# A gated windowed-attention and stream-mixing kernel: TensorE's chunk laid out anew, scores and values in the middle of a unit, the division one unit later, output parts in halves, gelu's low part on GpSimd and the normalisation on ScalarE

## The chip, the cores and the metric

One core of one Trainium2 chip runs the whole program. The metric is the device time in microseconds of one execution; a few executions of the same kernel are timed, and one more is recorded by the hardware profiler.

## What is computed

The input x is 8 x 512 x 2048 (batch, channels, positions). In short:

```
x = x + tanh(g_xattn) * attention(layernorm(x), ctx, mask)
x = x + tanh(g_ffn)  * mix(layernorm(x))
```

Attention works in windows of 128 positions: q and k from the normalised x, v from ctx (512 channels to 256), 8 heads of 32, softmax over 128 keys, exact gelu on the result, then a projection back to 512 channels. The mixing part takes each row's 2048 positions as four streams of 512. From 24 logits per row it makes a softmax for reading (pre), a softmax for writing (post) and, by 50 Sinkhorn iterations on a 4 x 4 matrix in logarithms, a mixing matrix. The output is the mixed streams plus post times the product of the read stream with a 512 x 512 matrix.

```
def step(carry, _):
    u, v = carry
    u = -jax.nn.logsumexp(Z + v[..., None, :], axis=-1)
    v = -jax.nn.logsumexp(Z + u[..., :, None], axis=-2)
```

## The kernel before

**Tiles and steps.** A chunk G is 512 positions of one batch element (32 chunks). It has four windows of two head groups each, which makes eight units. One batch element is a stage of 32 units, and there are 256 units in all. Every engine runs its own hand-written program, a loop over steps g with one unit per step; what stands in a step is set by tables of offsets within the chunk (`NORM_AT`, `HI_X_AT`, `LOW_X_AT`, `HI_CTX_AT`, `LOW_CTX_AT`, `T_AT`, ...). r is the step's number in its chunk, 0 to 7. Engines meet only through semaphores, and each engine works strictly in the order written.

**One unit.** TensorE makes the scores of unit g (`scores`, into the one bank `s_ps`), then the transposed scores less the maximum of unit g-1 (`scores_t`, bank `st_ps`), then the values of unit g-2 (`values`, bank `av_ps`), then the step's large products through a ring of four PSUM banks (`banked_at`). VectorE takes the maximum (`maximum`, L1003); ScalarE the exponential (`exp_scores`, L806) and the reciprocal of the denominator as exp(-ln) (`inverse_den`, L813 and L815); VectorE divides (`divide`, L1011). `values` of a unit waits for the division of the unit before it.

**Precision by halves.** The bf16 operands are pairs of a high and a low part. ScalarE makes the high part of x and ctx (`hi_x`, `hi_ctx`), GpSimd the low part by a subtraction (`split_x` L473, `split_ctx` L478); GpSimd also normalises x in place (`norm_x` L467). The high part of gelu's result is ScalarE's (`hi_gelu`), the low part VectorE's (`low_gelu` L1027). q and k are copied by 24 DMAs of the SP queue per chunk into stacked tiles `q_st` and `k_st`, before the chunk's first scores.

**The balance (Sinkhorn).** For a finished batch element, 98 half iterations run beside the units of the next one, up to four per step: VectorE sums `kp` and takes the reciprocal (`half_iteration`, L1135 and L1136), GpSimd multiplies `ke` by it into `kp` (`scale`, L533), VectorE sums again. In a step the four halves are spread between VectorE's other work: the maximum stands ahead of half 0; the reads of banks, the division and gelu's low part between halves 0 and 1; the output parts between 1 and 2; mask and statistics between 2 and 3. In GpSimd's program `split_x` stands between its scales 0 and 1, `norm_x` between 1 and 2, `split_ctx` between 2 and 3.

**The output.** 32 tiles of 128 rows. A tile's rows are reloaded (`load_x1t`), the read stream is made by ScalarE and three VectorE operations (`make_xpre`, L1168), transposed and multiplied on TensorE (`transpose_pre`, `branch`, L729), and the output tile `otile` is built: ScalarE's first products (`first_out`), three streams added for each of four columns (`add_stream`, L1180, two operations together), and the branch (`add_y`, L1193, four together). There is one `otile`; `first_out` waits until the tile before is stored. A tile starts every eight steps, from `TILE_AT`, also in the tail behind the last unit.

```
if 0 <= g < NU:
    scores(g)
if 0 <= g - 1 < NU:
    scores_t(g - 1)
if 0 <= g - 2 < NU:
    values(g - 2)
for what in banked_at(g):
    bank_free(what)
```

## Time and profile before

| what | value |
|---|---|
| median of 3 runs | 1891.67 us (1890.44 to 1893.29) |
| the profiled execution's own time | 1890.67 us |
| its span | 1888.8 us |
| TensorE busy | 1383.0 us, 73% |
| VectorE busy | 1437.9 us, 76% |
| ScalarE busy | 945.7 us, 50% |
| GpSimd busy | 824.0 us, 44% |
| first and last maximum (first and last unit on VectorE) | 68.5 us, 1595.7 us |

Busy time is the union of an engine's instructions, so an instruction that stands still while it waits for a port counts as busy. The profile's names: PE is TensorE, PEld its weight loads, DVE VectorE, ACT ScalarE, POOL GpSimd, SP the engine whose queue issues most DMAs. An arrow in brackets behind a row names what ended the engine's idle time before it.

### The profile page before, as it was taken

The numbers are of one execution on the slowest core, as the hardware profiler recorded it, in microseconds if no ns is written. First come the engines' busy times: TensorE is split into PE (matmuls) and PEld (weight loads), VectorE is DVE, ScalarE is ACT, GpSimd is POOL, SyncE is SP. The second block draws the span as 40 slices with busy tenths as digits, with TensorE's granted clock in tenths as the row PEclk, the third lists the DMA queues.
The fourth block names the chain that finished last, engine by engine and source line by source line (L and its number), as shares of the span: only waits on it lengthen the run. The fifth ranks groups of instructions, "written<-read, shape, count | busy, mean of one in ns | idle before, by whom it ended". The sixth has DMA issues, their size and how long they took to land. (4 is left out here: it accounts for less than half of the span.)

```text
span 1888.8 us, 35318 instructions
## 1 busy us (share of the span) xinstructions
PE 1383.0 (73%) x12301; PEld 848.2 (45%) x12448; DVE 1437.9 (76%) x3684; ACT 945.7 (50%) x1889; POOL 824.0 (44%) x1397
## 2 busy tenths in 40 slices
PE   2788999889978787888888887878888876431133
PEld 0555656556544454545544454445454544210011
DVE  3344555777788888888888888888788888777789
ACT  2445675555655555554655565554655554321112
POOL 4433334555454544555455545555464523323210
PEclk9889999989999999999999899999999997665567
DMA  7456765566666666666666666666655443421123
GB/s 248 145 146 184 207 192 159 161 175 180 174 180 183 185 165 170 187 189 169 176 173 182 169 190 176 177 171 178 171 169 150 134 120 93 121 73 60 56 89 123
DMA packets 173985, 299.80 MB, mean 159 GB/s; under 512 B 23664, under 2 KB 74736, under 8 KB 169712
## 3 DMA queue, kind: packets, MB, share of 16 engines
q1 hardware_dynamic: 156400, 263.97, 44.8%
q0 software_dynamic: 17408, 33.56, 11.1%
q8 instruction: 100, 1.64, 0.3%
q14 instruction: 77, 0.63, 0.1%
HBM read 179.75 MB, written 67.11 MB: 131 GB/s over the span
## 5 line engine op out<-in xcount | busy, mean ns | idle before, releaser
L533 POOL TENSOR_TENSOR kp<-ke,sv 128x64 f32<-128x64 f32 x376 | 183.4, 488 | 299.9 <-DVE sv L1136 299.8
L1135 DVE TENSOR_REDUCE ssum<-kp 128x16 f32<-128x64 f32 x768 | 181.8, 237 | 172.0 <-POOL kp L533 166.6
L533 POOL TENSOR_TENSOR kp<-ke,sa 128x64 f32<-128x64 f32 x392 | 125.8, 321 | 358.9 <-DVE sa L1136 358.9
L806 ACT ACTIVATE probs<-st_ps,key_bias 128x512 f32<-128x512 f32 x256 | 174.3, 681 | 199.6 <-PE st_ps L703 193.8
L605 PE MATMUL pr<-x_hl,wk 128*128 128x512 bf16 x736 | 194.2, 419 | 64.6 <-DVE k_hl L983 63.8
L1003 DVE TENSOR_REDUCE negm<-s_ps 128x4 bf16<-128x512 f32 x256 | 167.7, 655 | 75.6 <-PE s_ps L689 73.0
L605 PE MATMUL pr<-x_hl,wq 128*128 128x512 bf16 x707 | 187.0, 411 | 44.8 <-POOL x_hl L473 38.1
L473 POOL TENSOR_TENSOR x_hl<-xc,x_hl 128x512 bf16<-128x512 f32 x128 | 156.3, 1222 | 134.2 <-ACT x_hl L774 133.7
L619 PE MATMUL pr<-wv,ctx_hl 128*128 128x256 bf16 x1536 | 190.8, 284 | 24.0 <-POOL ctx_hl L478 24.0
L478 POOL TENSOR_TENSOR ctx_hl<-ctx_raw,ctx_hl 128x512 bf16<-128x512 f32 x128 | 176.4, 1378 | 57.4 <-ACT ctx_hl L768 57.4
L689 PE MATMUL s_ps<-k_st,q_st 97*128 97x128 bf16 x1024 | 102.8, 224 | 112.6 <-DVE negm L1003 101.0
L632 PE MATMUL pr<-o_sb,wo 128*128 128x512 bf16 x714 | 177.2, 386 | 4.1 <-issue 1.3
L619 PEld LDWEIGHTS pr<-wv,ctx_hl 128*128 128x128 bf16 x1536 | 152.3, 102 | 58.1 <-issue 36.1
L689 PEld LDWEIGHTS s_ps<-k_st,q_st 97*128 97x128 bf16 x1024 | 74.1, 100 | 189.8 <-DVE negm L1003 124.4
L701 PE MATMUL st_ps<-q_st,k_st 96*128 96x128 bf16 x1024 | 150.0, 223 | 7.3 <-ACT probs L806 4.4
L605 PEld LDWEIGHTS pr<-x_hl,wk 128*128 128x128 bf16 x768 | 79.3, 106 | 158.2 <-DVE k_hl L983 63.0
L703 PE MATMUL st_ps<-id_bf,negm 128*128 128x128 bf16 x1024 | 149.4, 223 | 0.0
L1011 DVE TENSOR_TENSOR o_sb<-av_ps,rden 128x128 f32<-128x128 f32 x256 | 70.4, 275 | 103.3 <-ACT rden L815 102.8
L716 PE MATMUL av_ps<-probs,v_t 128*32 128x128 f32 x2048 | 111.9, 290 | 41.0 <-DVE o_sb L1011 39.7
L605 PEld LDWEIGHTS pr<-x_hl,wq 128*128 128x128 bf16 x768 | 75.0, 104 | 141.3 <-issue 39.9
L729 PE MATMUL f<-wb,xpt 128*128 128x512 f32 x256 | 132.0, 664 | 8.5 <-ACT xpt L885 8.5
L676 PE MATMUL pr<-id_sb,xpre 128*128 128x128 f32 x128 | 24.1, 321 | 154.3 <-DVE xpre L1168 154.3
(139 smaller groups left out, 3031.7 us busy)
## 6 DMA issues: line engine op xcount, KB each, us to landing
xs<-in_dram SPq DMA_DIRECT2D x128, 256.0 KB, 4.0
xc<-in_dram SPq DMA_DIRECT2D x32, 1024.0 KB, 5.9
ctx_raw<-in_dram SPq DMA_DIRECT2D x32, 1024.0 KB, 5.1
x1c<-in_dram POOLq DMA_DIRECT2D x64, 512.0 KB, 5.9
x_dram<-x1c SPq DMA_DIRECT2D x32, 1024.0 KB, 4.3
out_dram<-otile SPq DMA_DIRECT2D x64, 512.0 KB, 5.0
q_st<-q_hl SPq DMA_DIRECT2D x384, 64.0 KB
k_st<-k_hl SPq DMA_DIRECT2D x384, 64.0 KB
```

What stands on the lines that cost most here:

```text
L473: nc.gpsimd.tensor_tensor(x_hl[:, G % 2, 1, t, :], xc[:, t, :], x_hl[:, G % 2, 0, t, :], ALU.subtract).then_inc(x_split, 1)
L478: ins = nc.gpsimd.tensor_tensor(ctx_hl[:, 1, t, :], ctx_raw[:, t, :], ctx_hl[:, 0, t, :], ALU.subtract)
L533: nc.gpsimd.tensor_tensor(kp[:], ke[:], v, ALU.mult).then_inc(kp_made, 1)
L605: ins = nc.tensor.matmul(bank(what)[:], w[:, a, t, i * P:(i + 1) * P], x_hl[:, G % 2, m, t, :], start=(t == 0 and a + m == 0), stop=(t == ...
L619: ins = nc.tensor.matmul(bank(what)[:, j * E:(j + 1) * E], ctx_hl[:, a, t, win], wv[:, m, t, :], start=(t == 0 and a + m == 0), stop=(t == ...
L632: ins = nc.tensor.matmul(bank(what)[:], wo[:, a, et, t * P:(t + 1) * P], o_part(G, et, m), start=(et == 0 and a + m == 0), stop=(et == ET ...
L689: ins = nc.tensor.matmul(s_ps[:, h * W:(h + 1) * W], q_st[0:ROWS + 1, G % 2, et, h, win], k_st[0:ROWS + 1, G % 2, et, h, win], start=True, ...
L701: nc.tensor.matmul(part, k_st[0:ROWS, G % 2, et, h, win], q_st[0:ROWS, G % 2, et, h, win], start=True, stop=False)
L703: ins = nc.tensor.matmul(part, negm[:, k % 2, h:h + 1].broadcast_to([P, P]), id_bf[:], start=False, stop=True)
L806: nc.scalar.activation(probs[:, k % 2, :], st_ps[:], ACT.Exp, bias=key_bias[:, b % 2, w:w + 1], scale=SCALE).then_inc(exp_done, 1)
L1003: nc.vector.tensor_reduce(negm[:, k % 2, :], s_ps[:].rearrange("p (h j) -> p h j", h=HPT), AX.X, ALU.max, negate=True).then_inc(max_done, 1)
L1135: cf.link(nc.vector.tensor_reduce(s_t, k, AX.X, ALU.add))
```

## The change

- **TensorE.** In a step `scores_t(g - 1)` comes first, then the first large product, then `scores(g + 1)` (a unit earlier than before) and `values(g - 2)`, then the other products. `branch` is two halves in two steps, `select` two halves in two steps. The transposes of x1 move from r = 2, 3 to 3, 4, the logits from 4 to 7, the transposes of the read stream from 3 to 1, the branch from 4 to 5 and 6.
- **VectorE.** `divide` is for unit g-3 and stands ahead of the bank reads. `add_stream` is one column at a time: one operation between halves 1 and 2, one between 2 and 3; `add_y` two and two; `make_xpre` two and one. `low_gelu` goes. The mask rows are made once for all chunks.
- **GpSimd.** `split_x` moves from between scales 0 and 1 to between 1 and 2; `norm_x` goes to ScalarE, ahead of each `hi_x`; `low_gelu` comes in at r = 3, one part ahead of scale 2 and one ahead of scale 3. The tables put `split_ctx` at r = 0, 1, 1, 4 (before 1, 2, 3, 5), and its first three parts now in steps in which ScalarE makes high parts of ctx too (0, 0, 1, 1).
- **ScalarE.** `norm_x` as above; `inverse_den` behind the first bank read.
- **Output and tail.** Two `otile` buffers. The tiles of the first six batch elements start one step later than before in the chunk; those of the last two start every six steps, with a denser table (`BEHIND`). The Sinkhorn steps begin one step later.
- **SP queue.** `store_x1` moves from r = 0 to 1; the separate mask loads of each stage go.

```diff
-NORM_AT, HI_X_AT, LOW_X_AT = [2, 3, 4, 5], [3, 4, 5, 6], [4, 5, 6, 7]
-HI_CTX_AT, LOW_CTX_AT = [0, 0, 1, 4], [1, 2, 3, 5]
-
-T_AT, LOGITS_AT, SELECT_AT = [2, 2, 3, 3], 4, 6
-STAT_B_AT = [2, 4]
+HI_X_AT, LOW_X_AT = [1, 4, 5, 6], [2, 5, 6, 7]
+HI_CTX_AT, LOW_CTX_AT = [0, 0, 1, 1], [0, 1, 1, 4]
+
+T_AT, LOGITS_AT, SELECT_AT = [3, 3, 4, 4], 7, 8
+STAT_B_AT = [1, 3]
...
+BESIDE = dict(load=-8, first=-6, xpre=-5, pre=-4, branch_0=0, branch_1=1, out_0=-1, out_1=0,
+              stream_1=0, stream_2=1, y=2, stream_3=4, pair_1=5, pair_2=6, pair_3=7, store_0=5, store_1=8)
+BEHIND = dict(load=-5, first=-3, xpre=-3, pre=-2, branch_0=-1, branch_1=-1, out_0=-1, out_1=0,
+              stream_1=0, stream_2=1, y=2, stream_3=3, pair_1=3, pair_2=4, pair_3=5, store_0=4, store_1=6)
+LAST_BESIDE = B - 3
+TILE_AT = {(f, t): UNITS * (f + 1) + 53 + UPC * t for f in range(LAST_BESIDE + 1) for t in range(DT)}
+TILE_AT.update({(B - 2, t): NU + SINK_AT - 1 + 6 * t for t in range(DT)})
+TILE_AT.update({(B - 1, t): NU + SINK_AT + len(SINK) + 1 + 6 * t for t in range(DT)})
...
             for g in range(FIRST, LAST):
-                if 0 <= g < NU:
-                    scores(g)
                 if 0 <= g - 1 < NU:
                     scores_t(g - 1)
-                if 0 <= g - 2 < NU:
-                    values(g - 2)
-                for what in banked_at(g):
-                    bank_free(what)
+                made = banked_at(g)
+                for n, what in enumerate(made):
...
+                    if n == 0:
+                        if 0 <= g + 1 < NU:
+                            scores(g + 1)
+                        if 0 <= g - 2 < NU:
+                            values(g - 2)
...
+                scale_at(f, its, 1)
                 for H, t in at_step(g, -2, LOW_X_AT):
                     split_x(H, t)
-                scale_at(f, its, 1)
-                for H, t in at_step(g, -2, NORM_AT):
-                    norm_x(H, t)
+                if 0 <= G - 1 < NG and r == 3:
+                    low_gelu(G - 1, 0)
                 scale_at(f, its, 2)
+                if 0 <= G - 1 < NG and r == 3:
+                    low_gelu(G - 1, 1)
...
+            def output_parts(g, half):
+                for j in range(1, N):
+                    for done, t in tiles_at(g, f"stream_{j}"):
+                        add_stream(done, t, j, half)
+                for done, t in tiles_at(g, "y"):
+                    add_y(done, t, half)
+                for j in range(1, N):
+                    for done, t in tiles_at(g, f"pair_{j}"):
+                        add_stream(done, t, j, 2 + half)
+                for done, t in tiles_at(g, "xpre"):
+                    make_xpre(done, t, half)
```

**Where the order moves.** TensorE, step r = 4 of a chunk in a steady stage, before (line numbers of the kernel before; L716 and L720 are the values, L659 the logits, L632 the output projection, L729 the whole branch, L689 the next unit's scores):

```order
L703 MATMUL st_ps<-id_bf,negm 128x128
L716 MATMUL av_ps<-probs,v_t 32x128 x4
L720 MATMUL av_ps<-probs,ones 32x128 x4
L659 MATMUL pr<-xt,wf 32x512 x4
L632 MATMUL pr<-o_sb,wo 128x512 x12
L729 MATMUL f<-wb,xpt 128x512 x4
L689 MATMUL s_ps<-k_st,q_st 128x128 x4
```

and changed, the end of step 4's transposed scores left out, steps 5 and 6 (L637 the output projection, L697 scores, L724 and L728 values, L739 the branch, L624 v):

```order
L637 MATMUL pr<-o_sb,wo 128x512 x6
L697 MATMUL s_ps<-k_st,q_st 128x128 x4
L724 MATMUL av_ps<-probs,v_t 32x128 x4
L728 MATMUL av_ps<-probs,ones 32x128 x4
L637 MATMUL pr<-o_sb,wo 128x512 x6
L739 MATMUL f<-wb,xpt 128x512 x2
```

The branch is cut in two and has left the step that also held the logits; scores and values now stand behind the step's first product.

VectorE, step r = 4, before: the halves of the balance are L1135 and L1136, both columns of a stream (L1180) stand in one gap, and mask row (L996) and statistics (L1044) in the next:

```order
L1003 TENSOR_REDUCE negm<-s_ps 128x4
L1135 TENSOR_REDUCE ssum<-kp 128x16
L1136 RECIPROCAL sa<-ssum 128x16
L983 SCALAR_TENSOR_TENSOR k_hl<-pr,bk_sb,k_hl 128x512
L1011 TENSOR_TENSOR o_sb<-av_ps,rden 128x128
L1135 TENSOR_REDUCE ssum<-kp 128x16
L1136 RECIPROCAL sv<-ssum 128x16
L1180 SCALAR_TENSOR_TENSOR otile<-x1t_even,cmat,otile 128x512 x2
L1135 TENSOR_REDUCE ssum<-kp 128x16
L1136 RECIPROCAL sa<-ssum 128x16
L996 TENSOR_SCALAR neg_row<-maskbc 1x512
L1044 BN_STATS bn_b<-x1c 128x6 x2
```

and changed (L1160 and L1161 the halves, L1207 the stream, L1005 a piece of the next element's statistics):

```order
L1034 TENSOR_REDUCE negm<-s_ps 128x4
L1160 TENSOR_REDUCE ssum<-kp 128x16
L1161 RECIPROCAL sa<-ssum 128x16
L1042 TENSOR_TENSOR o_sb<-av_ps,rden 128x128
L1019 SCALAR_TENSOR_TENSOR k_hl<-pr,bk_sb,k_hl 128x512
L1160 TENSOR_REDUCE ssum<-kp 128x16
L1161 RECIPROCAL sv<-ssum 128x16
L1207 SCALAR_TENSOR_TENSOR otile_even<-x1t_even,cmat,otile_even 128x512
L1160 TENSOR_REDUCE ssum<-kp 128x16
L1161 RECIPROCAL sa<-ssum 128x16
L1207 SCALAR_TENSOR_TENSOR otile_even<-x1t_even,cmat,otile_even 128x512
L1005 BN_STATS bn_a<-xs 128x6
```

The pair of stream operations is now one in each of two gaps, and the division comes ahead of the bank read.

GpSimd, the end of step r = 1 and steps 2 and 3, changed (L536 is the scale of the balance, L476 the low part of ctx, L471 that of x, L482 that of gelu):

```order
L476 TENSOR_TENSOR ctx_hl<-ctx_raw,ctx_hl 128x512 x2
L536 TENSOR_TENSOR kp<-ke,sa 128x64
L536 TENSOR_TENSOR kp<-ke,sv 128x64
L536 TENSOR_TENSOR kp<-ke,sa 128x64
L471 TENSOR_TENSOR x_hl<-xc,x_hl 128x512
L536 TENSOR_TENSOR kp<-ke,sv 128x64
L536 TENSOR_TENSOR kp<-ke,sa 128x64
L536 TENSOR_TENSOR kp<-ke,sv 128x64
L536 TENSOR_TENSOR kp<-ke,sa 128x64
L482 TENSOR_TENSOR o_sb<-g_sb,o_sb 128x512
L536 TENSOR_TENSOR kp<-ke,sv 128x64
L482 TENSOR_TENSOR o_sb<-g_sb,o_sb 128x512
```

Two parts of ctx now stand together in the last gap of step 1; the part of x has moved one scale later, behind scale 1; gelu's two parts each stand ahead of a scale in step 3.

## Rows read from the trace of the kernel before

**Rows 1.** The page: span, and busy time of each engine.

```profile
span 1888.8 us, 35318 instructions
PE 1383.0 (73%) x12301; PEld 848.2 (45%) x12448; DVE 1437.9 (76%) x3684; ACT 945.7 (50%) x1889; POOL 824.0 (44%) x1397
```

**Rows 2.** Windows: steady stages (20 chunks), tail; columns PE, PEld, DVE, ACT, POOL busy.

```profile
576.00:1596.00 1020.00, 828.68 (x7528) 507.58 (x7624) 867.16 (x2253) 573.48 (x1151) 501.54 (x840) 0.94 0.60 168
1596.00:1889.00 293.00, 87.50 (x263) 43.31 (x264) 230.32 (x583) 58.10 (x97) 65.05 (x172) 0.61 0.26 86
```

**Rows 3.** Waits of VectorE, 576 to 1596 us: total us, times, longest.

```profile
DVE ssum L1135 <- POOL kp L533: 84.2, 138, 1.7
DVE o_sb L1011 <- ACT rden L815: 33.1, 28, 2.4
DVE negm L1003 <- PE s_ps L689: 4.4, 10, 1.1
```

**Rows 4.** Groups by line, whole run: busy us, mean ns, idle before.

```profile
L478 POOL TENSOR_TENSOR ctx_hl<-ctx_raw,ctx_hl 128x512 bf16<-128x512 f32 x128 | 176.4, 1378 | 57.4 <-ACT ctx_hl L768 57.4
L473 POOL TENSOR_TENSOR x_hl<-xc,x_hl 128x512 bf16<-128x512 f32 x128 | 156.3, 1222 | 134.2 <-ACT x_hl L774 133.7
L1027 DVE TENSOR_TENSOR o_sb<-g_sb,o_sb 128x512 bf16<-128x512 f32 x64 | 44.4, 735 | 4.6 <-ACT o_sb L831 4.6
L996 DVE TENSOR_SCALAR neg_row<-maskbc 1x512 bf16<-1x512 f32 x32 | 17.9, 560 | 0.4 <-issue 0.2
L774 ACT ACTIVATE x_hl<-xc 128x512 bf16<-128x512 f32 x128 | 79.4, 621 | 6.5 <-POOL xc L467 6.4
```

**Rows 5.** Timeline of VectorE, 1802 to 1804 us: two halves with nothing between.

```profile
1802.12 0.26 DVE L1135 TENSOR_REDUCE ssum<-kp 128x16 f32<-128x64 f32 x1 [0.41 <-POOL kp L533]
1802.42 0.25 DVE L1136 RECIPROCAL sv<-ssum 128x16 f32<-128x16 f32 x1
1804.00 0.27 DVE L1135 TENSOR_REDUCE ssum<-kp 128x16 f32<-128x64 f32 x1 [0.41 <-POOL kp L533]
```

**Rows 6.** Timeline, 851 to 854 us: VectorE's stream pair first, GpSimd behind.

```profile
851.16 1.37 DVE L1180 SCALAR_TENSOR_TENSOR otile<-x1t_even,cmat,otile 128x512 f32<-128x512 f32 x2
851.33 0.65 POOL L533 TENSOR_TENSOR kp<-ke,sv 128x64 f32<-128x64 f32 x1 [0.19 <-DVE sv L1136]
851.94 1.60 POOL L478 TENSOR_TENSOR ctx_hl<-ctx_raw,ctx_hl 128x512 bf16<-128x512 f32 x1
```

**Rows 7.** Timeline, 903 to 906 us: GpSimd's large operation first.

```profile
903.29 1.16 POOL L478 TENSOR_TENSOR ctx_hl<-ctx_raw,ctx_hl 128x512 bf16<-128x512 f32 x1
903.73 1.94 DVE L1180 SCALAR_TENSOR_TENSOR otile<-x1t_odd,cmat,otile 128x512 f32<-128x512 f32 x2
```

**Rows 8.** Timeline of ScalarE and VectorE around gelu, 317 to 323 us.

```profile
317.32 1.28 ACT L819 ACT_TABLE_LOAD   x1
321.43 0.67 ACT L806 ACTIVATE probs<-st_ps,key_bias 128x512 f32<-128x512 f32 x1
322.51 1.13 ACT L831 ACTIVATE o_sb<-g_sb 128x512 bf16<-128x512 f32 x2
322.64 0.29 DVE L1011 TENSOR_TENSOR o_sb<-av_ps,rden 128x128 f32<-128x128 f32 x1 [4.17 <-ACT rden L815]
```

**Rows 9.** Timeline of TensorE, 289 to 299 us: select and v in one step.

```profile
289.58 4.40 PE L668 MATMUL pr<-sti,lgs 128*128 128x32 f32 x32
293.79 5.31 PE L619 MATMUL pr<-wv,ctx_hl 128*128 128x256 bf16 x24
```

**Rows 10.** Timeline of VectorE, tail: `add_y` beside the balance (two), behind it (two).

```profile
1709.44 2.63 DVE L1193 SCALAR_TENSOR_TENSOR otile<-f,post,otile 128x512 f32<-128x512 f32 x4
...
1748.66 2.63 DVE L1193 SCALAR_TENSOR_TENSOR otile<-f,post,otile 128x512 f32<-128x512 f32 x4
...
1837.46 2.73 DVE L1193 SCALAR_TENSOR_TENSOR otile<-f,post,otile 128x512 f32<-128x512 f32 x4 [0.34 <-PE f L729]
...
1851.23 2.73 DVE L1193 SCALAR_TENSOR_TENSOR otile<-f,post,otile 128x512 f32<-128x512 f32 x4 [0.22 <-PE f L729]
```

More of the change, by code:

```diff
@@ L661, in logits, with select @@
                 ins.then_inc(bank_full, 1)
-            def select(what):
+            def select(what, part):
                 kind, f, i = what
-                pe.wait_ge(lg_copied, NC * (f + 1))
-                for t in range(DT):
+                if part == 0:
+                    pe.wait_ge(lg_copied, NC * (f + 1))
+                for t in (2 * part, 2 * part + 1):
                     for w in range(NC):
@@ L1188, in add_y @@
[L1188 to L1199 removed]
+                if half:
+                    ins.then_inc(xpre_ready, 1)
```

284 lines of the change are left out of this document (143 added, 141 removed).

## The prediction

> **What bounds the kernel now.** I read the page first [rows 1]: no engine is full, VectorE is the busiest with 76% and TensorE next with 73%, so the limit differs by stage and has to be read there. The windows [rows 2] show two regimes. From 576 to 1596 us (chunks 11 to 30, every engine at work) VectorE is busy 867.2 of 1020 us. That is 43.4 us per chunk of 51.0, with 7.6 us idle. GpSimd is busy 501.5, so neither it nor ScalarE (573.5) is near full. The tail, from 1596 us, has only VectorE busy, 230.3 of 293 us. The waits of VectorE in the steady part [rows 3] say what the 7.6 us are: 84.2 us (4.2 per chunk) for GpSimd's scale of the balance, 33.1 us (1.7) for ScalarE's reciprocal before the division, and only 4.4 us for TensorE's scores. So the bound is VectorE together with its ping-pong with GpSimd. TensorE waits for them, and a smoother TensorE gives time only where it paces: in the first chunks.
>
> **The ping-pong.** With nothing between, two halves take 1804.00 - 1802.12 = 1.88 us [rows 5], of which 0.41 each is idle. Work of VectorE in the gap behind a half is free up to about 0.4 us. A large GpSimd operation ahead of the scale costs where VectorE has too little to cover it.
>
> **Two engines, one port.** Where VectorE's stream pair comes first, GpSimd's part of ctx takes 1.60 us and ends 1.01 us after the pair [rows 6]. Where GpSimd comes first it takes 1.16, and the pair 1.94 instead of 1.37 [rows 7], though VectorE had nothing else in hand. So a stream operation, which reads two tiles from SBUF, and a large GpSimd operation do not run together. The Trainium skill (SBUF — State Buffer, Who interferes with whom) says that a VectorE instruction with two SBUF inputs contends with a GpSimd one that reads SBUF, and that the loser fully blocks. By that rule the trace agrees: 1.60 against 1.16 us.
>
> **The change, part by part, per steady chunk.**
>
> *Work that VectorE loses.* Two low parts of gelu of 0.735 us and one mask row of 0.56 [rows 4]: 2.0 us by duration. Successive instructions overlap by about 0.1 each, so I take 1.65. Left: 43.4 - 1.65 = 41.75. The streams, the read stream and the branch are the same operations, only parted.
>
> *Waits that go.* The division is for unit g-3, so ScalarE has a whole unit more: the 1.7 us go. The part of x (1.16 to 1.22) leaves the gap that holds only the division or a bank read, and the normalisation leaves GpSimd. That is most of today's 4.2 us, and I count all of it anew.
>
> *Waits that come*, in a chunk with the balance in all eight steps. Gaps that now hold the division alone, r = 7 and 0: 0.3 each. The scale that starts behind a single stream operation must let it finish: about 0.15 in five gaps, 0.75. Part of x behind a short bank read, r = 2: it ends about 0.5 after the stream operation wants the port, 0.5. At r = 5 and 6 two bank reads cover it, at r = 7 the branch reads PSUM. Part of ctx at r = 4, now ahead of a stream operation: 0.65. DMA issue at r = 6: 0.1. Then three places where GpSimd takes what ScalarE makes in the same step, which it did not before. At r = 0 the high part of ctx stands on ScalarE behind exponential, bank read and reciprocal, each of which waits for TensorE; I put its end 5.5 us into the step, where GpSimd wants it at 4.0, and with the port 1.65 in all. At r = 1 two parts stand together, the second made about 6.0 us into the step, 2.05. At r = 3 the low part of gelu: table loads, gelu and exponential take 322.10 - 317.32 = 4.8 us, the first high part 0.6 more [rows 8]; begun 2.7 us into step 2 (5.7 us long), that is about 8.1, where GpSimd wants it at 7.1; with the port and the second part 1.95. Sum 0.6 + 0.75 + 0.5 + 0.65 + 0.1 + 1.65 + 2.05 + 1.95 = 8.25. The balance runs in 26 of 32 steps, which makes 6.7; 0.7 for the softmax steps and what else waits now. Together 7.4, against 7.6 today.
>
> Step lengths and ScalarE's times in it are my placement; no row shows them. Bounds: ScalarE is in time everywhere (3.4 less at full, 2.8 on the mean), or each of the three is later by another 0.8 us (a reciprocal and a bank read), 2.0 more on the mean. I take the middle because step r = 3 shows today that ScalarE falls behind by 4.17 us at the gelu [rows 8].
>
> *Steady sum:* 41.75 + 7.4 = 49.15 against 51.0, -1.85 per chunk. Chunks 8 to 31, 24 of them: **-44 us**.
>
> *ScalarE* gets four normalisations per chunk; the nearest row is its copy of the same shape, 0.62 us [rows 4]: 2.5 us of 51, from 56% busy [rows 2] to about 62%. Nothing for them, since none stands at r = 2 or 3; if that cover went, they would delay the exponential by 1.2 us at their steps. *SP queue:* the q and k stacks must be there half a unit earlier, behind the load of a tile and `store_x1` a step later. TensorE waits for scores inputs nowhere in [rows 3] beyond 4.4 us; zero. *PSUM ring and branch halves:* zero in the steady part, TensorE has 828.7 of 1020 us [rows 2].
>
> *First eight chunks* (TensorE paces from the second to the sixth). Select 4.40 and v 5.31 us stand in one step there [rows 9]; halves of select in two other steps give back about 4 once. The wait of 4.17 us at gelu [rows 8] shrinks by perhaps 1 per chunk, since values now stand later in the step. **-10 us**, between 0 and -25.
>
> *Tail.* Beside the balance a tile takes 1748.66 - 1709.44 = 39.2 us in eight steps [rows 10], now six steps, each with more in it; the balance runs its own steps at the pace of [rows 5] whatever else stands there, and single stream operations hide a little more of the 0.41 us. A tile of the second last element that stood behind the balance is now beside it: nothing to -5 us. Against it, at the end: today ten stream operations lie between read stream and branch and TensorE is awaited for 0.22 to 0.34 us [rows 10]; now eight do, 1.43 us less cover, three times: +4.5. And the balance begins a step later: +4. **+6 us**, between -10 and +15.
>
> Sum: 1890.67 - 44 - 10 + 6 = 1842.7 for the profiled execution; the median stands 1.0 above it: **1844 us**.
>
> **Rivals.**
>
> *The port and ScalarE decide, slower.* A chunk has ten large GpSimd operations: four of x, four of ctx, two of gelu. I charge 3.1 us of blocking for them. If each blocks the operation that VectorE has next by 0.7 us (its 1.16 less the 0.45 of a half), that is 7.0: +3.9 per chunk, x 24 = +94, **1938 us**. It decides from +2.0 per chunk, 0.5 us for each of the ten. For it: the pair of 1.94 us [rows 7], and that one of the two streams now stands in every gap behind which GpSimd works. Against: at r = 5, 6 and 7 there is cover. The Trainium skill (Perfetto Trace Analysis, Optimizing Scalar/DVE Operations) warns that moving operations between VectorE and GpSimd might not help, since they share a read port; it speaks against gelu's low part on GpSimd.
>
> *The waits nearly vanish.* ScalarE is in time and the ports overlap well: 3.4 us per chunk of waits instead of 7.4. -4.0 x 24 = -96: **1748 us**. For it: today 7.6 us of idle time come from a few gaps. Against: at least 2.1 us of what I list hang on no placement.
>
> *A wash.* The steady chunk keeps its 51.0 because what goes returns elsewhere: -10 + 6, **1888 us**. For it: 7.4 against 7.6 is nearly that already, and VectorE's lost 1.65 us may only bare a wait for GpSimd, for gelu's low part covers one today.
>
> **How the numbers follow.** Forecast (1810 to 1878) 0.52, slower by the port 0.18, waits vanish 0.16, wash 0.14. The range takes the unknowns: 24 x 2.8 = 67 below and 24 x 2.0 = 48 above, with the tail: 1785 to 1900. It leaves out most of the slower rival and the far part of the fast one, together under 0.2. Differences under 0.2% (3.8 us) can't be told from none. Of the wash 0.06 is faster, 0.06 the same, 0.02 slower: faster 0.74, same 0.06, slower 0.20.
>
> **What would show it.** VectorE's wait for ScalarE's reciprocal gone from its list; its wait for the scale about 6 us per chunk and longest at r = 0, 1 and 3; GpSimd waiting for ScalarE's high part of ctx and of gelu; VectorE busy about 42 us per chunk; a steady chunk of 49 us; 1.5 us waits for the branch in the last three tiles. Wrong if TensorE is what VectorE waits for in the steady part, if the chunk stays at 51, or if it falls below 47.

## The result, and the profile after

The changed kernel takes **1884.14 us** (median of 5 runs, 1878.06 to 1888.89), the kernel before 1891.1 in the same comparison: ratio 0.9947, interval 0.9925 to 0.9969. That is 10 us less by the ratio, where 47 were forecast. The profiled execution took 1878.06 us, the fastest of the five and 6 us under their median, so terms of a few us below are not sure. Of run 7 below, one of six executions took 4650.91 us; its ratio leaves that one out. Where the time lies, by the first maximum of a unit: the first maximum comes 2.5 us later (71.0 for 68.5), chunks 0 to 7 take 307.8 us against 318.8 (-11.0, forecast -10), chunks 8 to 31 take 1201.4 against 1208.4 (**-7.0, forecast -44**), and from the last maximum to the end it is 296.0 against 293.1 (+2.9, forecast +6). So one term failed, the steady one.

The page of the changed kernel (its first lines), answering to [rows 1]:

```profile
span 1876.2 us, 35394 instructions
PE 1423.7 (76%) x12448; PEld 859.5 (46%) x12448; DVE 1390.8 (74%) x3582; ACT 1055.6 (56%) x2017; POOL 799.5 (43%) x1333
```

VectorE lost 47 us of work, ScalarE gained 110, and TensorE's busy time rose by 41 us though it computes the same (147 matmul records of large products are missing from the trace of before, but an output product with one missing is busy 2.77 us there and a whole one 2.76, so they explain little of that). For the steady part I take chunks 8 to 27, the same 20 chunks in every kernel from here on. The windows view, before (first line) and after (second); columns: time, PE, PEld, DVE, ACT, POOL busy, TensorE's granted clock, DMA share, GB/s:

```profile
387.30:1406.60 1019.30, 837.15 (x7648) 513.83 (x7744) 853.59 (x2248) 578.68 (x1168) 517.19 (x871) 0.95 0.63 176
```

```profile
378.80:1388.10 1009.30, 866.38 (x7750) 521.97 (x7749) 823.93 (x2178) 647.29 (x1244) 495.50 (x831) 0.93 0.62 177
```

VectorE's work fell by 29.7 us, 1.48 per chunk (forecast 1.65). Its idle time rose from 165.7 to 185.4 us, that is from 8.3 to 9.3 per chunk. What it waits for there (total, times, longest), answering to [rows 3]:

```profile
DVE ssum L1160 <- POOL kp L536: 120.1, 187, 4.3
DVE ssum L1160 <- ACT ke L892: 21.0, 10, 3.2
DVE q_hl L1019 <- ACT q_hl L819: 8.2, 5, 2.4
...
DVE o_sb L1042 <- ACT rden L846: 1.4, 2, 1.2
```

The wait for the reciprocal is gone, as forecast (36.7 us before in the same chunks). The wait for the scale has grown from 89.4 us, and it is one place: ahead of the fourth half of step r = 1 VectorE stands idle 3.09 us in the mean of the 15 such steps that hold the balance; it is 1.16 at r = 0 (15 steps) and 1.46 ahead of the third half at r = 3 (10 steps). Of GpSimd, ScalarE and TensorE (same view, same chunks) these have grown or are new:

```profile
ACT lnden L844 <- PE av_ps L728: 122.5, 108, 3.2
...
POOL ctx_hl L476 <- ACT ctx_hl L792: 113.4, 38, 6.1
PE s_ps L697 <- DVE negm L1034: 107.8, 68, 3.2
POOL o_sb L482 <- ACT o_sb L862: 77.0, 20, 7.8
```

Before, TensorE's wait for the maximum was 77.3 us and ScalarE's for the values 18.8. In exchange ScalarE's wait for the transposed scores fell from 118.6 to 12.5, and TensorE's for VectorE's read of q and k, 55.1 before, is gone. Both engines wait less in sum (TensorE is idle 142.9 us instead of 182.1), but elsewhere. Read from the bottom of the chain: VectorE waits for GpSimd, GpSimd for ScalarE, ScalarE for TensorE, and TensorE for VectorE. One step r = 1 shows the whole ring (the timeline; start, length, engine; in brackets idle time before and its releaser):

```profile
929.40 0.63 PE L684 MATMUL pr<-id_sb,xpre 128*128 128x128 f32 x4 [0.69 <-DVE xpre L1195]
...
931.35 0.63 DVE L1034 TENSOR_REDUCE negm<-s_ps 128x4 bf16<-128x512 f32 x1
...
932.03 0.61 PE L697 MATMUL s_ps<-k_st,q_st 97*128 97x128 bf16 x4 [2.00 <-DVE negm L1034]
...
932.67 0.65 PE L724 MATMUL av_ps<-probs,v_t 128*32 128x128 f32 x8
...
933.55 0.66 DVE L1207 SCALAR_TENSOR_TENSOR otile_even<-x1t_even,cmat,otile_even 128x512 f32<-128x512 f32 x1
...
933.69 5.09 PE L610 MATMUL pr<-x_hl,wq 128*128 128x512 bf16 x12
...
934.33 1.15 POOL L476 TENSOR_TENSOR ctx_hl<-ctx_raw,ctx_hl 128x512 bf16<-128x512 f32 x1
...
934.83 1.20 DVE L1207 SCALAR_TENSOR_TENSOR otile_even<-x1t_even,cmat,otile_even 128x512 f32<-128x512 f32 x1
...
938.82 0.69 ACT L819 ACTIVATE q_hl<-pr,bq_sb 128x512 bf16<-128x512 f32 x1 [4.39 <-PE pr L610]
...
939.08 2.75 PE L610 MATMUL pr<-x_hl,wk 128*128 128x512 bf16 x12
939.40 1.14 ACT L792 ACTIVATE ctx_hl<-ctx_raw 128x512 bf16<-128x512 f32 x2
940.10 1.17 POOL L476 TENSOR_TENSOR ctx_hl<-ctx_raw,ctx_hl 128x512 bf16<-128x512 f32 x1 [4.62 <-ACT ctx_hl L792]
...
941.55 0.27 DVE L1160 TENSOR_REDUCE ssum<-kp 128x16 f32<-128x64 f32 x1 [4.33 <-POOL kp L536]
```

At r = 1 the first bank product is only the read stream's transposes. Behind them stand the scores of the next unit, which need the maximum of this one, since both use the one tile `s_ps`. TensorE stands idle 2.00 us until VectorE starts the step. Only then come values and the q product, ScalarE's read of it 7.5 us into the step (938.82 - 931.35), the high part of ctx behind that, GpSimd's low part, the scale, and VectorE's half. The step takes 10.7 us. The q product takes 5.09 us where the k product behind it, of the same shape, takes 2.75. The granted clock says why (windows view):

```profile
929.50:930.60 1.10, 0.53 (x4) 0.28 (x4) 0.36 (x1) 1.10 (x3) 1.10 (x2) 1.00 1.09 207
930.60:931.35 0.75, 0.00 (x0) 0.00 (x0) 0.44 (x3) 0.33 (x1) 0.24 (x1) 1.00 0.39 77
931.35:932.00 0.65, 0.00 (x0) 0.00 (x0) 0.65 (x3) 0.00 (x0) 0.30 (x1) 0.71 0.02 3
932.00:933.69 1.69, 1.63 (x21) 1.01 (x21) 1.62 (x7) 0.00 (x0) 0.30 (x1) 0.50 0.43 164
933.69:938.60 4.91, 4.91 (x16) 1.78 (x13) 3.31 (x6) 0.59 (x2) 1.76 (x2) 0.52 0.92 317
939.08:941.80 2.72, 2.72 (x15) 1.08 (x12) 0.24 (x1) 2.69 (x5) 1.42 (x2) 1.00 0.01 3
```

Full level (2.4 GHz) before the idle time, a fall within it, half (1.2 GHz) behind it and through nearly all of the q product. In the mean of the 20 chunks the clock is 0.86 at r = 1 and 0.73 at r = 3 (before: 0.95 and 0.84).

### The profile page after: what moved, and what is told of

Its sections match the earlier page's. It is cut to its first block, busy times and chain, and to the rows that moved or that the text cites. A ratio compares the mean times of both kernels' runs of the same rounds, so it can differ in the third digit from the quotient of the medians.

```text
span 1876.2 us, 35394 instructions
## 1 busy us (share of the span) xinstructions
PE 1423.7 (76%) x12448; PEld 859.5 (46%) x12448; DVE 1390.8 (74%) x3582; ACT 1055.6 (56%) x2017; POOL 799.5 (43%) x1333
## 4 chain that ended last, share of the span: by engine, by line
PE 43%; DVE 22%; POOL 11%; ACT 10%; issue 9%; DMA 2%; SPq 2%; DVEq 0%; POOLq 0%; ACTq 0%
PE pr L610 11%; PE pr L624 7%; PE pr L637 6%; POOL kp L536 5%; PE f L739 4%; DVE ssum L1160 4%; PE av_ps L724 4%; POOL ctx_hl L476 3%; DVE otile_odd L1207 3%; DVE negm L1034 2%; PE av_ps L728 2%; SPq L404 2%; DVE sa L1161 2%; PE s_ps L697 2%; DVE sv L1161 1%
## 5 line engine op out<-in xcount | busy, mean ns | idle before, releaser
L1160 DVE TENSOR_REDUCE ssum<-kp 128x16 f32<-128x64 f32 x768 | 181.8, 237 | 208.3 <-POOL kp L536 206.1
L536 POOL TENSOR_TENSOR kp<-ke,sa 128x64 f32<-128x64 f32 x392 | 158.0, 403 | 283.8 <-DVE sa L1161 283.8
L536 POOL TENSOR_TENSOR kp<-ke,sv 128x64 f32<-128x64 f32 x376 | 166.2, 442 | 226.7 <-DVE sv L1161 225.7
L476 POOL TENSOR_TENSOR ctx_hl<-ctx_raw,ctx_hl 128x512 bf16<-128x512 f32 x128 | 149.6, 1174 | 217.3 <-ACT ctx_hl L792 217.3
L610 PE MATMUL pr<-x_hl,wq 128*128 128x512 bf16 x768 | 205.8, 426 | 35.1 <-POOL x_hl L471 35.1
L1034 DVE TENSOR_REDUCE negm<-s_ps 128x4 bf16<-128x512 f32 x256 | 167.0, 652 | 74.7 <-PE s_ps L697 73.2
L697 PE MATMUL s_ps<-k_st,q_st 97*128 97x128 bf16 x1024 | 104.4, 226 | 151.3 <-DVE negm L1034 138.4
L637 PE MATMUL pr<-o_sb,wo 128*128 128x512 bf16 x768 | 188.0, 389 | 8.8 <-POOL o_sb L482 6.6
L471 POOL TENSOR_TENSOR x_hl<-xc,x_hl 128x512 bf16<-128x512 f32 x128 | 148.5, 1160 | 92.8 <-ACT x_hl L805 92.8
L624 PE MATMUL pr<-wv,ctx_hl 128*128 128x256 bf16 x1536 | 183.0, 277 | 3.1 <-DVE wv L1244 3.1
L844 ACT ACTIVATE lnden<-av_ps 128x128 f32<-128x128 f32 x256 | 71.0, 277 | 196.5 <-PE av_ps L728 191.4
L697 PEld LDWEIGHTS s_ps<-k_st,q_st 97*128 97x128 bf16 x1024 | 71.7, 100 | 221.7 <-DVE negm L1034 153.4
L624 PEld LDWEIGHTS pr<-wv,ctx_hl 128*128 128x128 bf16 x1536 | 148.7, 99 | 28.3 <-issue 9.8
L1207 DVE SCALAR_TENSOR_TENSOR otile_even<-x1t_even,cmat,otile_even 128x512 f32<-128x512 f32 x192 | 147.8, 780 | 1.6 <-ACT otile_even L925 1.2
L1207 DVE SCALAR_TENSOR_TENSOR otile_odd<-x1t_odd,cmat,otile_odd 128x512 f32<-128x512 f32 x192 | 148.4, 795 | 0.7
L724 PE MATMUL av_ps<-probs,v_t 128*32 128x128 f32 x2048 | 117.1, 302 | 36.1 <-DVE o_sb L1042 35.2
L739 PE MATMUL f<-wb,xpt 128*128 128x512 f32 x256 | 138.8, 677 | 5.5 <-ACT xpt L916 5.5
## 6 DMA issues: line engine op xcount, KB each, us to landing
xc<-in_dram SPq DMA_DIRECT2D x32, 1024.0 KB, 10.7
```

The lines of the kernel that those rows point to most:

```text
L476: ins = nc.gpsimd.tensor_tensor(ctx_hl[:, 1, t, :], ctx_raw[:, t, :], ctx_hl[:, 0, t, :], ALU.subtract)
L536: nc.gpsimd.tensor_tensor(kp[:], ke[:], v, ALU.mult).then_inc(kp_made, 1)
L610: ins = nc.tensor.matmul(bank(what)[:], w[:, a, t, i * P:(i + 1) * P], x_hl[:, G % 2, m, t, :], start=(t == 0 and a + m == 0), stop=(t == ...
L624: ins = nc.tensor.matmul(bank(what)[:, j * E:(j + 1) * E], ctx_hl[:, a, t, win], wv[:, m, t, :], start=(t == 0 and a + m == 0), stop=(t == ...
L637: ins = nc.tensor.matmul(bank(what)[:], wo[:, a, et, t * P:(t + 1) * P], o_part(G, et, m), start=(et == 0 and a + m == 0), stop=(et == ET ...
L697: ins = nc.tensor.matmul(s_ps[:, h * W:(h + 1) * W], q_st[0:ROWS + 1, G % 2, et, h, win], k_st[0:ROWS + 1, G % 2, et, h, win], start=True, ...
```

## The experiments

Each run is told as median, ratio to the kernel before in the same comparison, and interval. Theory A took the handover within a step for the cause, as the forecast had it; TensorE's order came in with run 7. A gap is the part of VectorE's step between two halves of the balance, and its wait is the idle time ahead of the half that ends it. Differences between runs are of medians; by the ratios they are the same within 4 us. A number for a gap or a clock by step is the mean over the steps of that r in the 20 chunks (for gaps, over those that hold the balance).

### 1. The parts of ctx a step later

```diff
-HI_CTX_AT, LOW_CTX_AT = [0, 0, 1, 1], [0, 1, 1, 4]
+HI_CTX_AT, LOW_CTX_AT = [0, 0, 1, 1], [1, 2, 4, 5]
```

> Changed kernel with GpSimd's low parts of ctx at r = 1, 2, 4, 5 instead of 0, 1, 1, 4, so that none waits for a high part that ScalarE makes in the same step. Theory A (handover in the same step): in the changed kernel VectorE waits about 3.1 us in one gap of r = 1 and 1.2 in one of r = 0, and GpSimd waits 113 us for the high part of ctx in 20 chunks. This takes about 2.5 us per chunk away and gives 0.7 back at the new places: -1.8 x 24 = -43, about 1841 us. Theory B (the time lost there is slack that the next wait takes, TensorE's order or ScalarE's answers): 1875 to 1888 us, VectorE's wait for the scale falls but another wait grows.

**1827.98 us**, 0.9649 (0.9637 to 0.9662): 56 us faster than the changed kernel. Its waits in the 20 chunks:

```profile
DVE ssum L1160 <- POOL kp L536: 60.2, 159, 2.6
...
POOL ctx_hl L476 <- ACT ctx_hl L792: 30.4, 5, 6.1
...
DVE ssum L1160 <- ACT ke L892: 19.0, 10, 2.7
```

The wait for the scale is halved, the gaps at r = 0 and 1 are down to 0.01 and 0.00 us. Theory A holds as far as it goes: the wait is where it said. It doesn't tell why the high parts are late.

### 2 to 4. Three parts of the change undone, one at a time

The low part of gelu back on VectorE:

```diff
@@ GpSimd @@
-                if 0 <= G - 1 < NG and r == 3:
-                    low_gelu(G - 1, 0)
...
@@ VectorE @@
                         read_wo(what)
+                if 0 <= G - 1 < NG and r == 3:
+                    for et in range(ET):
+                        low_gelu(G - 1, et)
```

> Changed kernel with gelu's two low parts back on VectorE, behind the bank read of r = 3. Theory A (the chunk holds too many waits for GpSimd, the work taken from VectorE comes back as a wait): VectorE busy +1.4 us per chunk, wait at r = 3 -1.5 (its gap waits 1.46 us in the mean), the same time within 5 us. Theory B (the move of gelu's low part is itself a loss since GpSimd waits 77 us for ScalarE's high part in 20 chunks): faster by 15 to 30 us. Theory C (the move is a gain of its full duration): slower by 30 us.

1918.08 us, 1.0127 (1.011 to 1.0144): 34 us slower than the changed kernel, as theory C had it. But only 8 us are in the 20 steady chunks (1017.6 against 1009.3), where the wait at r = 3 went as theory A said, and 8 more in the four chunks behind them. Some 21 us are in the first eight chunks: chunk 8 begins at 400.4 us instead of 378.8, and VectorE waits there for ScalarE's `o_sb` (25.9 us up to that point) where the changed kernel has no such wait. That this holds up TensorE, which paces there, is my reading of it.

The normalisation back on GpSimd (`norm_x` between scales 1 and 2, at r = 1, 2, 4, 5):

```diff
@@ ScalarE @@
-                    norm_x(H, t)
                     hi_x(H, t)
@@ GpSimd @@
+                for H, t in at_step(g, -2, NORM_AT):
+                    norm_x(H, t)
```

> Changed kernel with the four normalisations of x per chunk back on GpSimd, between scales 1 and 2 of r = 1, 2, 4, 5. Theory A (ScalarE's lateness decides r = 1 and the steps where its answers stand last): ScalarE loses 2.5 us per chunk, most of it at r = 1, 4, 5, 6, but GpSimd's large operation stands between two scales again: VectorE's wait for the scale grows by about 0.5 us in each of four gaps, net +20 us. Theory B (the normalisation on ScalarE costs the changed kernel its gain): faster by 10 us or more.

1892.83 us, 1.0001 (0.9987 to 1.0016): 9 us slower. Neither theory's size, theory A's sign.

The output parts whole:

```diff
                 output_parts(g, 0)
-                half_at(f, its, 2)
                 output_parts(g, 1)
+                half_at(f, its, 2)
```

> Changed kernel with both single stream operations of a step in one gap again, as before. Theory A (halves let each gap hide a scale, 0.41 us of the two): the gap without a stream operation waits 0.4 us more, in some 22 steps per element and in the tail: slower by 40 to 60 us. Theory B (halves cost by blocking GpSimd's scale at the port in two gaps where it was one; they are part of the loss): faster by 10 us or more, the scale's mean time falls. If neither, within 5 us.

1902.93 us, 1.0047 (1.0033 to 1.0061): 19 us slower, 12 of them in the 20 chunks and 10 in the tail. The gaps without a stream operation wait 0.4 us again; r = 1 waits 3.72.

So none of the three is the loss; each is a gain.

### 5 and 6. Which handover

```diff
-HI_CTX_AT, LOW_CTX_AT = [0, 0, 1, 1], [0, 1, 1, 4]
+HI_CTX_AT, LOW_CTX_AT = [0, 0, 0, 0], [0, 1, 1, 4]
```

> Changed kernel with all four high parts of ctx made by ScalarE at r = 0, GpSimd's low parts where the change has them (r = 0, 1, 1, 4). At r = 1 GpSimd's pair of low parts then waits for nothing, but it is still a pair in one gap and still meets VectorE's stream operation at the port. Theory A (the wait for the high part made in the same step is the loss): about half to two thirds of what the run with later low parts gained over the changed kernel comes back, 1840 to 1850 us, and the gap of 3.09 us at r = 1 falls below 1. Theory P (two large GpSimd operations in one gap are the loss, port and length): little comes back, 1865 to 1880, and the gap stays above 2 us.

1856.13 us, 0.9793 (0.9773 to 0.9813): half of the first run's gain, a little short of theory A's 1840 to 1850. The gap at r = 1 is 0.17 us with the pair still in it: the pair isn't the loss, the wait is. r = 3 rises to 2.07.

```diff
-HI_CTX_AT, LOW_CTX_AT = [0, 0, 1, 1], [0, 1, 1, 4]
+HI_CTX_AT, LOW_CTX_AT = [0, 0, 1, 1], [0, 2, 4, 5]
```

> Low parts of ctx at r = 0, 2, 4, 5: against the run with 1, 2, 4, 5 only the first is moved, back into the step in which ScalarE makes its high part. It gives the price of that one handover. Theory A: the gap at r = 0 waits 1.16 us again, times 0.75 (balance present) times 24 = +21, with some of it given back at r = 1 where the gap is now free: 1828 + 12 to 21 = 1840 to 1849 us. Rival (the handover at r = 1 was all of it): within 4 us of 1828.

1864.18 us, 0.9835 (0.9813 to 0.9857): the one handover at r = 0 costs 36 us, more than the 12 to 21 expected. Of the 28.6 us in the 20 chunks 23.7 lie in the steps r = 0, where the gap is back at 1.38 us; 7.6 lie at r = 2, whose gap rises from 0.91 to 1.62 with nothing changed there. So a late step reached a later one, which handovers alone don't explain.

### 7. Scores, values and division as before, all else as changed

```diff
@@ TensorE @@
+                if 0 <= g < NU:
+                    scores(g)
                 if 0 <= g - 1 < NU:
                     scores_t(g - 1)
+                if 0 <= g - 2 < NU:
+                    values(g - 2)
...
-                            scores(g + 1)
...
-                            values(g - 2)
@@ ScalarE @@
                     exp_scores(g - 1)
+                if 0 <= g - 2 < NU:
+                    inverse_den(g - 2)
@@ VectorE @@
                 half_at(f, its, 0)
-                if 0 <= g - 3 < NU:
-                    divide(g - 3)
...
                         read_wo(what)
+                if 0 <= g - 2 < NU:
+                    divide(g - 2)
```

> Changed kernel with scores and values back at the start of TensorE's unit, ScalarE's reciprocal ahead of the bank reads and the division of unit g-2 behind them; its tables stay. Theory A (later division takes VectorE's wait for the reciprocal away, 1.7 us per chunk, and the loss lies with ctx): the wait for rden returns with 30 to 40 us in 20 chunks, and ScalarE's bank reads come later, so it is slower by 20 to 40 us, about 1915. Theory D (scores and values in mid unit delay ScalarE, so its high parts come too late: this order is the cause of the loss): faster than the changed kernel, 1850 to 1875 us.

**1786.26 us**, 0.9416 (0.9394 to 0.9437): 98 us faster than the changed kernel. Theory A expected it slower by 20 to 40, and falls as the root cause; theory D has the direction, and the gain is larger than its 1850 to 1875. The reciprocal's wait does return, with 24.4 us, and costs less than what goes. Its 20 chunks (windows):

```profile
368.60:1311.10 942.50, 818.30 (x7731) 504.11 (x7730) 832.16 (x2178) 637.04 (x1242) 513.29 (x831) 0.97 0.67 189
```

Its waits there, of VectorE and of TensorE:

```profile
DVE ssum L1152 <- POOL kp L536: 56.5, 163, 3.2
DVE o_sb L1034 <- ACT rden L840: 24.4, 31, 2.5
...
PE pr L684 <- DVE xpre L1187: 35.8, 17, 3.0
PE pr L637 <- DVE k_hl L1011: 34.1, 18, 3.0
PE pr L637 <- POOL o_sb L482: 20.2, 17, 1.5
PE s_ps L697 <- DVE negm L1026: 16.5, 15, 1.8
```

TensorE's wait for the maximum is 16.5 us instead of 107.8, its clock 0.97. Other waits of TensorE have come, so its idle time falls by only 18.7 us (142.9 to 124.2); its busy time falls by 48.1 (866.4 to 818.3) at the same work, and its time at half clock from 143 to 58 us, of which 74 went at r = 3 and 24 at r = 1. VectorE's idle time falls by 75.1 us (185.4 to 110.3). The same step as above (unit 153):

```profile
885.86 2.75 PE L610 MATMUL pr<-x_hl,wq 128*128 128x512 bf16 x12
...
887.04 0.63 DVE L1026 TENSOR_REDUCE negm<-s_ps 128x4 bf16<-128x512 f32 x1
...
888.45 0.39 PE L697 MATMUL s_ps<-k_st,q_st 97*128 97x128 bf16 x4
...
888.65 0.69 ACT L813 ACTIVATE q_hl<-pr,bq_sb 128x512 bf16<-128x512 f32 x1 [1.85 <-PE pr L610]
```

The q product takes 2.75 us, is begun 1.2 us before VectorE's step and read 1.6 us into it, not 7.5. The step takes 6.4 us instead of 10.7; in the mean of the 20 chunks r = 1 takes 6.8 instead of 9.4.

### 8 and 12. The handovers moved too, in the new and in the old order

```diff
-HI_CTX_AT, LOW_CTX_AT = [0, 0, 1, 1], [0, 1, 1, 4]
+HI_CTX_AT, LOW_CTX_AT = [0, 0, 1, 4], [1, 2, 4, 5]
@@ GpSimd @@
-                if 0 <= G - 1 < NG and r == 3:
-                    low_gelu(G - 1, 0)
                 scale_at(f, its, 2)
                 if 0 <= G - 1 < NG and r == 3:
-                    low_gelu(G - 1, 1)
+                    low_gelu(G - 1, 0)
...
                 scale_at(f, its, 3)
+                if 0 <= G - 1 < NG and r == 3:
+                    low_gelu(G - 1, 1)
```

> Low parts of ctx at r = 1, 2, 4, 5, the fourth high part at r = 4 instead of 1, and gelu's two low parts one scale later in r = 3. What waits longest in the run with low parts at 1, 2, 4, 5 is the scale behind gelu's first part (0.99 us) and behind the part of x at r = 2 (0.91 us). Theory A (the wait is for what ScalarE makes in the same step): both fall by half, about -0.6 us per chunk with the balance there, 1828 - 12 = 1816 us. Rival (TensorE's o projection at r = 4 needs gelu's last part, and the first chunks, where TensorE paces, lose what the later ones gain): 1828 or slower.

1805.39 us, 0.9527 (0.9507 to 0.9547); the gap at r = 3 falls from 0.99 to 0.21 us, 23 us gained on the first run where theory A had 12.

> Old order of scores, values and division, with the low parts of ctx at r = 1, 2, 4, 5, the fourth high part at r = 4 and gelu's low parts one scale later. If the two losses (the order, and the handover in the same step) are one (ScalarE late because TensorE is), the second brings little on top: the gaps at r = 0 and 1 wait only 0.53 and 0.56 us with the old order, 0.6 us per chunk to gain: 1770 to 1782 us. If they are independent, 1884 - 98 - 79 = 1710.

**1766.71 us**, 0.9332 (0.9318 to 0.9347), faster than both kernels and than any other run: 127 us under the kernel before, by the ratio. Its gain on run 7 is 20 us, not 79: the two losses are mostly one. Its 20 chunks:

```profile
366.10:1292.20 926.10, 805.64 (x7656) 499.25 (x7734) 832.75 (x2177) 637.30 (x1244) 513.67 (x831) 0.98 0.68 192
```

and VectorE's waits in them:

```profile
DVE ssum L1152 <- POOL kp L536: 43.7, 159, 0.9
DVE o_sb L1034 <- ACT rden L840: 21.7, 23, 2.7
```

A chunk takes 46.3 us, 41.6 of them work and 4.7 idle.

### 9 to 11. Which part of the order

Division of g-3 with values at the start of the unit:

> Changed kernel with TensorE's and ScalarE's order of before (scores and values at the start of the unit), but the division still for unit g-3, right behind the first half. Undoing order and division together gave 1786 us against 1884. Theory V (the single PSUM tile of the values is the loop: values of g-2 wait for the division of g-3, which the change puts into VectorE's step g, so TensorE and ScalarE can't run ahead): most of the loss stays, 1850 to 1890 us. Theory S (TensorE's place for scores is the loss: the scores of g+1 wait for the maximum of unit g and hold everything behind them on TensorE): nearly all is back, 1780 to 1800 us.

2141.98 us, 1.1306 (1.1282 to 1.1331). That is +356 on run 7: theory V's direction, at four times its middle, and theory S's 1780 to 1800 is far off. TensorE's longest wait in the 20 chunks:

```profile
PE av_ps L724 <- DVE o_sb L1034: 313.1, 158, 6.6
```

There is one PSUM tile for the values. Those of g-2 wait for the division of g-3, and put first in TensorE's unit they hold all of it.

Scores and values in mid unit with the division of before:

> Changed kernel with only the division as before (unit g-2, behind the bank reads); scores and values stay in mid unit. Theory S (scores in mid unit hold the bank products and values behind VectorE's maximum, so ScalarE and GpSimd are late): no better than the changed kernel, 1880 to 1920 us, since VectorE now also waits for the reciprocal. Theory V (division later is the loop): faster, 1800 to 1850 us.

2063.26 us, 1.089 (1.0867 to 1.0914), +179 on the changed kernel: both theories missed, S by 140 us in its own direction. VectorE's longest wait:

```profile
DVE o_sb L1042 <- ACT rden L846: 215.9, 149, 4.2
```

The two halves of the edit need each other: either without the other is the dearest thing in this study.

Only the scores in mid unit, the rest of the order as before:

> Changed kernel with values at the start of TensorE's unit, ScalarE's reciprocal early and the division of unit g-2, as before; only the scores of g+1 stay behind the first bank product. Against the run with all of the old order (1786 us) only the scores are moved. Theory S: 60 to 100 us slower, 1845 to 1885, and TensorE's wait for the maximum at the scores (16.5 us in 20 chunks there, 107.8 in the changed kernel) returns. Theory V, or values in mid unit as the loss: within 10 us of 1786.

1848.61 us, 0.9754 (0.9736 to 0.9772): +62 on run 7, with TensorE's wait for the maximum back:

```profile
PE s_ps L697 <- DVE negm L1030: 101.8, 82, 3.2
```

Of the 98 us, 62 come with the scores, and 36 more with values, reciprocal and division.

### 13 and 14. The level table, and the division a gap later

Both on run 12.

```diff
-T_AT, LOGITS_AT, SELECT_AT = [3, 3, 4, 4], 7, 8
+T_AT, LOGITS_AT, SELECT_AT = [2, 2, 3, 3], 4, 8
```

> The run with the old order of scores, values and division and the later low parts (1767 us), with the transposes of x and the logits back at the steps of before (2, 2, 3, 3 and 4; the change has 3, 3, 4, 4 and 7); select stays. The levelled table was to help where TensorE paces, in the first chunks only. Theory L (levelling is a small gain in the first chunks): 5 to 10 us slower, with unit 64 reached later and the 20 chunks behind it the same. Rival M (the level table is what lets VectorE's next maximum find its scores in the steady part too): 20 us or more slower. Rival N: within 4 us.

1802.78 us, 0.9525 (0.9511 to 0.9539): +36. Theory L's 8 us are there (chunk 8 begins at 374.2 instead of 366.1), but 22.6 more lie in the 20 chunks, where the wait for the reciprocal doubles to 41.7 us. So it is rival M by its size; the wait that grew is the one for the reciprocal, while VectorE's wait for scores, which M named, is 1.9 us.

```diff
-                if 0 <= g - 2 < NU:
-                    divide(g - 2)
                 half_at(f, its, 1)
+                if 0 <= g - 2 < NU:
+                    divide(g - 2)
```

> The same run (1767 us) with the division of unit g-2 behind the second half instead of ahead of it. Its only wait beside the scale is 21.7 us in 20 chunks for the reciprocal. Theory A (a little more distance takes that wait, and nothing waits for the division yet): -10 to -20 us, 1750 us. Theory V (the values of the next unit wait for this division: a later one holds TensorE, as the division of g-3 in the first gap of step g did at +356 us): TensorE's wait for the division grows from a few us, and the time is 1767 or more, up to 1800.

1776.7 us, 0.9385 (0.9368 to 0.9402): +10. The wait for the reciprocal doesn't fall (25.6 us). TensorE's wait for the division doubles, from 11.5 us (run 12) to 23.5. Theory V, in small.

### 15 to 18. The wait itself taken away, the order kept

A second tile for the scores, with one tile less in the ring; each beside a control with the smaller ring only.

```diff
-RING = 4
+RING = 3
...
-        s_ps = ps("s_ps")
+        s_ps = [ps("s_ps_even"), ps("s_ps_odd")]
...
-                if k:
-                    pe.wait_ge(max_done, k)
+                if k >= 2:
+                    pe.wait_ge(max_done, k - 1)
...
```

On the changed kernel, control and run:

> Changed kernel with three PSUM tiles in the ring of bank products instead of four, nothing else: the control for the next run. TensorE has to wait for an earlier read of a bank: slower than 1884 by 10 to 100 us.

> Changed kernel with three tiles in the ring and the free one as a second tile for the scores, so that the scores of g+1 in mid unit wait for the maximum of g-1, not of g. The order on every engine stays that of the change. Theory S (the wait of the scores for the maximum is what the mid-unit place costs: TensorE idles 2 us at r = 1, its granted clock falls, 0.86 in the mean there and 0.73 at r = 3, and the bank product behind it comes 2.3 us later still): against the control 50 us faster or more, TensorE's wait for the maximum (107.8 us in 20 chunks) nearly gone and the granted clock at r = 1 and 3 above 0.9. Theory O (the place alone, more work ahead of the bank product, is the cost, the wait only fills slack): within 15 us of the control.

1897.63 us, 1.0031 (1.0018 to 1.0044), and 1906.67, 1.007 (1.0045 to 1.0095). A miss for theory S: 9 us slower, not 50 faster. TensorE's waits tell why, control first:

```profile
PE s_ps L697 <- DVE negm L1034: 101.3, 63, 3.2
...
PE av_ps L724 <- DVE o_sb L1042: 14.2, 46, 1.6
```

```profile
PE av_ps L724 <- DVE o_sb L1042: 130.2, 71, 3.6
```

The wait for the maximum is gone and one for the division stands in its place: in the changed kernel it stands two operations behind the maximum. The clock stays low (0.80 at r = 1, 0.83 in the control). With values and division as before (run 11) that second lock isn't there:

> The run with only the scores in mid unit (values, reciprocal and division in the old order, 1849 us), with three ring tiles instead of four: control for the next. On the changed kernel the fourth tile was worth 13 us; expected 1850 to 1880.

> The same with the free PSUM tile as a second one for the scores. In the run on the changed kernel a second score tile took the wait for the maximum away, and TensorE waited at the values for the division of g-3 instead (130.2 us in 20 chunks, 14.2 in its control), which stands right behind the maximum there. Here the values come at the start of the unit and their division is done in VectorE's step before, so nothing is left to take that wait's place. Theory S2 (two locks at one moment: TensorE waits in mid unit for VectorE's step g, by the maximum or by the division): 30 to 60 us faster than the control, near the 1786 us of the old order plus the price of the tile. Theory O (the place in the list is the cost, not a wait): within 10 us of the control.

1884.75 us, 0.9949 (0.9933 to 0.9965), and **1840.4**, 0.9717 (0.9693 to 0.974): 44 us faster in the same order. Waits in the 20 chunks, control first:

```profile
ACT q_hl L817 <- PE pr L610: 154.1, 40, 8.7
...
PE s_ps L697 <- DVE negm L1030: 92.8, 69, 3.2
```

```profile
ACT q_hl L817 <- PE pr L610: 125.5, 40, 8.7
...
PE st_ps L709 <- DVE negm L1030: 9.7, 8, 1.5
```

At the scores TensorE waits for no maximum any more (9.7 us are left at the transposed scores), and its clock at r = 1 rises from 0.81 to 0.88. So it is the wait, and not the place as such. The control was slower than expected: the fourth bank is worth 36 us in this order (1884.75 against run 11's 1848.61), not the 13 of run 15. That is also most of what keeps run 18 from run 7. Of the 36.4 us that it takes longer in the 20 chunks, 29.4 lie at r = 2 (6.43 us a step against 4.96), where the control has the same loss against run 11 (6.37 against 4.82). At r = 1 it is level with run 7 (6.81 and 6.75 us), at r = 3 too (6.98 and 6.99).

## Why the prediction was wrong

- **Base, limit, first eight chunks, tail:** right in size. -11.0 for -10, +2.9 for +6. That the -10 came by the forecast's two reasons isn't shown: VectorE's wait for the reciprocal fell there from 60.4 to 44.2 us and its wait for scores rose from 67.3 to 73.2; neither is traced to one of them. Gelu on GpSimd, forecast as a gain of steady work only, is worth some 21 us there (run 2). So the sum hides terms of both signs, and that it fits is in part luck. In the tail VectorE waits 7.6 us for the branch instead of 0.7, more than the 4.5 forecast, and the total is still below the forecast.
- **Work that VectorE loses:** -1.48 per chunk for -1.65. The sum is right, its items aren't. Gelu and mask give the 2.0 us, the read stream in parts 0.7 more; against it the stream operations became longer, from 726 and 753 ns to 823 and 838 by even and odd tile, 23.9 us of busy time in 20 chunks (146.5 to 170.4). I had priced the streams as "the same operations, only parted".
- **Waits that go:** right for the reciprocal (1.8 per chunk before in these 20, 0.1 now).
- **Waits that come:** 9.3 per chunk in place of 7.4 (and these chunks had 8.3 before, not 7.6: +1.0 where -0.2 was forecast). r = 0 with 1.16 (1.65 forecast) and r = 3 with 1.46 (1.95) are near. **r = 1 was priced at 2.05 and takes 3.09** of idle time alone, with stream operations up to 1.20 us long instead of 0.66 on top. The forecast had the second high part of ctx made 6.0 us into that step; in the step shown it ends about 8.7 us into it. Not in the list at all: 1.05 per chunk for ScalarE's answer `ke` (0.26 before), and 0.6 for its high parts of q and k.
- **The step that failed** is what these grew from: "The division is for unit g-3, so ScalarE has a whole unit more", "a smoother TensorE gives time only where it paces", and a zero for TensorE in the steady part, since it was busy only 828.7 of 1020 us. I costed the later division on VectorE's side and the scores in mid unit at nothing. But an engine with slack helps only if it may run ahead. Each of `s_ps` and `av_ps` is one tile, so TensorE has to meet VectorE once per tile and unit, and the change moved both meetings from the edge of TensorE's unit into its middle, ahead of bank products. Price: 98 us (run 7), 62 of them by the scores alone (run 11), and with a second tile for the scores 44 us of it are gone though the place stays (run 18).
- **The level table** (x1's transposes and logits in other steps) has no term of its own: the -10 names select and the wait at gelu. It gives 36 us on run 12, 23 of them in the steady chunks (run 13). The change as a whole is these and the other parts' gains (34, 9 and 19 us, runs 2 to 4, each alone and not to be added) against that price.
- **The range:** its lower end doesn't follow from its terms. 67 us below 1844 are 1777, and 1785 is given without a term for the difference.
- **Rivals.** The wash gave the number, 1888, and half its reason: what goes returns elsewhere. Where it returns wasn't named. "The waits nearly vanish", 1748, is near run 12 (1767), with 4.7 us idle per chunk for the 3.4 it names: what kept it off was mostly one edit of the change, TensorE's order with the division (run 7, 1786), and then the places of ctx and gelu. "The port and ScalarE decide", 1938, is refuted as a total, though the port's cost is real in the streams. The Trainium skill (SBUF — State Buffer, Who interferes with whom) has this port as an exclusive lock between the two engines; the trace agrees here as in [rows 6, 7]: a stream operation takes 0.66 us beside a scale and 1.20 beside a part of ctx. The Trainium skill's warning (Perfetto Trace Analysis, Optimizing Scalar/DVE Operations) that offloading between the two might not help isn't borne out for gelu: 34 us gained.

## What to carry to other kernels

Where an engine with spare time shares a single buffer with the limiting one, ask at which place of its list it has to meet that engine, and what stands behind that place: a product that could have run ahead is then late by a whole step. Two waits for the same moment hide each other, so taking one away shows nothing (run 16); take the second away as well (run 18). And a transfer of work between two engines in the same step is only as good as the third engine that feeds them: move the consumer a step later before judging it (56 us in run 1, and 20 with gelu's parts moved too once TensorE isn't late, run 12).
